# Mixture-of-experts tail on one core: one region of rows per expert, 39 tiles, and outputs added to memory by accumulating indirect DMAs

## The chip, the cores and the metric

One core of a Trainium2 (trn2) chip runs the whole program. The metric is the device time of one execution in microseconds (us), as the median of several runs. Engines are named as in the profile: PE (matmul), PEld (weight load), DVE, ACT, POOL and SP; a "q" behind a name is that engine's own instruction queue, which also issues DMAs.

## What is computed

Per batch of 512 rows (four batches, width 512), a linear attention over 1024 context rows, then a layer of eight experts, of which each row uses two:

```python
def _L0_ffn_ref(x, Wr, We, be):
    logits = jnp.einsum('bsd,de->bse', x, Wr)
    w, sel = jax.lax.top_k(logits, 2)
    w = jax.nn.softmax(w, axis=-1)
    gate = jnp.einsum('bsk,bske->bse', w, jax.nn.one_hot(sel, E, dtype=w.dtype))
    for e in range(E):
        out = out + gate[..., e:e + 1] * (jnp.einsum('bsd,df->bsf', x, We[e]) + be[e])

x = x + _L0_xattn_ref(_layernorm(x), ctx, Wq, Wg, bg, Wkv, Wo)
x = x + _L0_ffn_ref(_layernorm(x), Wr, We, be)
```

There are 2048 rows and so 4096 pairs of a row and an expert. Every matmul is in float32 precision, made of three passes over operands cut into a high and a low half (`three`: high by high, high by low, low by high).

## The kernel before, in words

**Attention.** Each engine has an instruction stream written by hand. The lists `KEYS` and `QUERIES` set the order of the steps of a batch. Batch by batch PE makes keys, values, queries, gate, attention and the output projection; DVE adds the residual into `x2`; POOL has the expert weights cut and stored in DRAM (`we_halves`) beside it. Two steps of batch b run within the keys of batch b+1: the logits with `pick_two` (the two experts of each row and their weights) and `rank_two` (the place of each pair among the pairs of its expert). POOL then scatters each normed row twice, by two indirect DMAs of 128 rows (`scatter`, L493), into `xs`: a region of rows per expert.

**Experts.** The pairs come in two groups, batches 0 to 2 and batch 3, with regions of their own. `plan` (DVE) works out on the device which expert and which rows each tile of 128 rows has: 31 tiles for group 0 and 15 for group 1, a fixed 46, enough for any routing. SP zeroes 128 rows behind each expert's last one (`pad`, eight stores per group). A tile goes through these steps:

- SP reads the tile's row from `tile_row`, waits for a free slot (two slots) and loads 128 rows (`load_tile`, L361).
- PE turns the tile (`turn_m`, L1165: four transposes); ACT copies out the high half (`high_m`, L716), DVE makes the low half (`low_m`, L810).
- PE does twelve matmuls of 512 columns (`expert`, L1098 to L1100).
- DVE adds the expert's bias into one of two slots of `y_sb` (`copy_y`, L1014), and ACT stores it to `y` in DRAM (`store_y`, L733).

The list `START` sets the order of the first 13 tiles, among which the normed rows of batch 3 are turned ("T", "z"), and their logits ("L") and places ("K") are made. After the last tile of group 0 is stored, POOL gathers the two expert rows of each token for 12 blocks of 128 tokens (`gather`, L598), DVE scales and adds both to the residual (`combine`, L1020 and L1024), ACT stores the block to the output (`store_out`, L737). These 12 blocks run beside the last 12 tiles. The four blocks of batch 3 come after the last tile.

**Loads before the experts.** In SP's queue stand, in this order: `load_halves(1)` to `(3)`, the eight pads, tiles 0 and 1, eight loads of the biases (L394), `load_halves(4)` and `(5)` (L374, 2 MB each, after the gate matmuls of the last batch), tile 2, tile 3, `load_halves(6)`, tile 4, `load_halves(7)`. POOL passes each arrival on (`halves_in`) to PE's `we_ready`.

## Time and profile before

| | |
|---|---|
| median of 3 runs | 607.82 us (605.88 to 607.92) |
| profiled execution: its own time | 602.09 us |
| its span on the core | 600.6 us |
| PE busy | 546.1 us (91%) |
| DVE, ACT, POOL busy | 320.0, 186.9, 166.9 us |
| DMA | 114.18 MB, mean 190 GB/s |
| mean granted TensorE clock | 0.968 |

The span runs from the first to the last instruction of the core; the profiled execution's own time is 1.49 us longer. PE's busy time is an overlap of pipelined matmuls, so the distance between starts says what one costs. All times within the trace are us from the span's start.

### The profile page before, as it was taken

To read this page: it belongs to the slowest core of one execution; us is meant where nothing else is said; L and a number is where in the kernel's file an instruction comes from. 1 tells how busy PE (TensorE), PEld (TensorE's weight loads), DVE (VectorE), ACT (ScalarE), POOL (GpSimd) and SP (SyncE) were. 2 spreads that over 40 slices of the span, in tenths; PEclk is the share of its full clock that TensorE was granted. 3 is DMA by queue.
4 is the path that set the end of the run, shared out by engine and by line. 5 is a ranking of instruction groups with operands and counts; after the bars stand their busy time and mean duration, and the time that the engine had idled before them with its cause. 6 is when DMAs were issued, how large, how long until landed. Compare 5 with 4: busy or idle time off the path is not lost.

```text
span 600.6 us, 12872 instructions
## 1 busy us (share of the span) xinstructions
PE 546.1 (91%) x4192; PEld 443.6 (74%) x4193; DVE 320.0 (53%) x857; ACT 186.9 (31%) x340; POOL 166.9 (28%) x194
## 2 busy tenths in 40 slices
PE   6999996999999999999999999994899999999850
PEld 4778785788878888877888887883678888877630
DVE  4463374356436727535746645770566544447744
ACT  5456321334532343443244343231111111111100
POOL 3014645403633131554040350010112000055413
PEclk9999999799999999999999999996899999999995
DMA  8813344632453062355052137789847568789946
GB/s 270 308 37 106 141 141 169 201 122 108 149 196 114 18 229 71 139 179 207 4 202 80 72 141 297 264 286 420 306 147 241 145 206 269 226 254 369 408 178 189
DMA packets 44446, 114.18 MB, mean 190 GB/s; under 512 B 4976, under 2 KB 4976, under 8 KB 43504
## 3 DMA queue, kind: packets, MB, share of 16 engines
q1 hardware_dynamic: 24240, 57.43, 28.6%
q0 software_dynamic: 11232, 39.85, 18.5%
q10 hardware_dynamic: 8928, 16.26, 7.1%
q8 instruction: 32, 0.52, 0.4%
q14 instruction: 14, 0.11, 0.1%
HBM read 66.86 MB, written 46.66 MB: 189 GB/s over the span
## 4 chain that ended last, share of the span: by engine, by line
PE 61%; DMA 12%; issue 5%; POOL 3%; SPq 3%; DVE 3%; ACT 1%; POOLq 0%; DVEq 0%; ACTq 0%
PE pj L1098 17%; PE pj L1100 17%; PE pj L1099 17%; DMA khat<-xs 5%; PE tp L1090 4%; PE tp L1165 3%; DMA out_dram<-wraw 1%; DMA wraw<-in_L_ffn_We_dram 1%; POOL aux L533 1%; PE pj L1185 1%; PE kvb L1157 1%; DMA we_halves<-aux 1%; PE pj L1107 1%; DMA qhat<-y,gidx 1%; SPq L365 1%
## 5 line engine op out<-in xcount | busy, mean ns | idle before, releaser
L1098 PE MATMUL pj<-R 128*128 128x512 f32 x448 | 185.6, 414 | 10.3 <-DVE R L806 9.3
L1100 PE MATMUL pj<-R 128*128 128x512 f32 x448 | 177.4, 396 | 0.0
L1099 PE MATMUL pj<-R 128*128 128x512 f32 x448 | 176.8, 395 | 0.0
L1098 PEld LDWEIGHTS pj<-R 128*128 128x128 f32 x448 | 85.4, 191 | 27.4 <-DVE R L806 10.3
L1100 PEld LDWEIGHTS pj<-R 128*128 128x128 f32 x448 | 85.2, 190 | 19.3
L1099 PEld LDWEIGHTS pj<-R 128*128 128x128 f32 x448 | 85.7, 191 | 15.4
L1098 PE MATMUL pj<-R,aux 128*128 x184 | 77.5, 421 | 5.5 <-issue 3.6
L1100 PE MATMUL pj<-R,aux 128*128 x184 | 73.2, 398 | 0.0
L1099 PE MATMUL pj<-R,aux 128*128 x184 | 73.0, 397 | 0.0
L716 ACT CAST aux<-tp 128x512 fp32r<-128x512 f32 x46 | 26.9, 585 | 121.6 <-PE tp L1165 114.5
L806 DVE TENSOR_TENSOR R<-tp,R 128x512 fp32r<-128x512 f32 x64 | 43.8, 684 | 24.9 <-ACT R L638 24.7
L871 DVE SCALAR_TENSOR_TENSOR khat<-buf,khat 128x512 f32<-128x512 f32 x32 | 25.1, 783 | 54.0 <-ACT buf L675 53.9
L500 POOL TENSOR_TENSOR rstd<-rstd,mhalf 128x1 f32<-128x1 f32 (+1 forms) x20 | 13.4, 669 | 126.7 <-DVE rstd L824 126.6
L1098 PEld LDWEIGHTS pj<-R,aux 128*128 128x128 f32 x184 | 35.4, 192 | 15.2 <-issue 9.0
L493 POOL DMA_INDIRECT xs<-normed,xidx x16 | 16.2, 1013 | 100.7 <-DVE xidx L859 98.3
L598 POOL DMA_INDIRECT qhat<-y,gidx x16 | 15.9, 995 | 95.2 <-issue 77.1
L810 DVE TENSOR_TENSOR aux<-tp,aux 128x512 fp32r<-128x512 f32 x46 | 31.7, 689 | 18.5 <-ACT aux L716 17.4
L1100 PEld LDWEIGHTS pj<-R,aux 128*128 128x128 f32 x184 | 35.3, 192 | 7.5
L1099 PEld LDWEIGHTS pj<-R,aux 128*128 128x128 f32 x184 | 35.4, 193 | 6.0
L638 ACT CAST R<-tp 128x512 fp32r<-128x512 f32 x64 | 37.7, 589 | 6.2 <-PE tp L1090 5.7
L1165 PE MATMUL tp<-ident,khat 128*128 128x128 f32 x184 | 28.6, 278 | 11.8 <-DMA khat<-xs 11.8
L533 POOL TENSOR_TENSOR aux<-wraw,aux 128x1024 fp32r<-128x1024 f32 x14 | 36.7, 2620 | 1.2
(158 smaller groups left out, 652.5 us busy)
## 6 DMA issues: line engine op xcount, KB each, us to landing
we_halves<-aux POOLq DMA_DIRECT2D x14, 1024.0 KB, 5.0
R<-we_halves SPq DMA_DIRECT2D x7, 2048.0 KB, 11.9
khat<-xs SPq DMA_DIRECT2D x46, 256.0 KB, 3.6
wraw<-in_L_ffn_We_dram POOLq DMA_DIRECT2D x16, 512.0 KB, 6.4
buf<-in_ctx_dram SPq DMA_DIRECT2D x15, 512.0 KB, 3.8
y<-kvbd ACTq DMA_DIRECT2D x23, 256.0 KB, 3.6
y<-zeros ACTq DMA_DIRECT2D x23, 256.0 KB
wraw<-in_x_dram SPq DMA_DIRECT2D x4, 1024.0 KB, 8.0
```

Source lines behind the costliest of these rows:

```text
L493: nc.gpsimd.indirect_dma_start(out=xs_dram[g][:, :], out_offset=bass.IndirectOffsetOnAxis(ap=xidx[:, t, j:j + 1], axis=0), in_=xn[t], in_o ...
L533: nc.gpsimd.tensor_tensor(aux[:, 2:4, :], e_raw[:, ks, :], aux[:, 0:2, :].bitcast(F32), ALU.subtract).then_inc(wx_low, 1)
L638: nc.scalar.copy(dst, src).then_inc(SEMS["h_" + kind], 1)
L716: nc.scalar.copy(xsT_hi[:, slot, :, :], tp[slot][:, :, :]).then_inc(MOE["h_m"], 1)
L806: nc.vector.tensor_tensor(lo, tp_bank("l_" + kind, i)[:, :, :], hi.bitcast(F32), ALU.subtract).then_inc(SEMS["l_" + kind], 1)
L810: nc.vector.tensor_tensor(xsT_lo[:, slot, :, :], tp[slot][:, :, :], xsT_hi[:, slot, :, :].bitcast(F32), ALU.subtract).then_inc(MOE["l_m"], 1)
L871: nc.vector.scalar_tensor_tensor(khat[:, i % 2, :], expk[:, i % 2, :], 1.0, khat[:, i % 2, :], ALU.min, ALU.add).then_inc(SEMS["khat"], 1)
L1090: last = nc.tensor.transpose(bank[:, k, :], src[:, k * P:(k + 1) * P], ident[:, :])
L1098: nc.tensor.matmul(bank[:, :], s_hi(k), m_hi(k), start=(k == 0), stop=False)
L1099: nc.tensor.matmul(bank[:, :], s_hi(k), m_lo(k), start=False, stop=False)
L1100: last = nc.tensor.matmul(bank[:, :], s_lo(k), m_hi(k), start=False, stop=(k == KT - 1))
L1165: last = nc.tensor.transpose(tp[slot][:, k, :], xs_raw[:, slot, k * P:(k + 1) * P], ident[:, :])
```

## The change

- `xs` is one region per expert for all four batches. A row is 528 floats wide: 512 values, the gates of the eight experts, the row's token number and a mark for padding. `x2_dram`, `y_dram`, the gathers, `combine` and `store_out` are gone. `store_x2` writes the residual straight into the output.
- There are 39 tiles. The first 17 (`M0`) are full ones from batches 0 to 2 (`plan_full`); `plan_rest` orders the other 22 when batch 3 is ranked. Pads are one block of 128 rows at the end of `xs` and one per expert.
- A tile's rows bring their gate and token: `pay` (DVE) takes the tile's expert from a table and copies the gate to `w_sel` and the token to `out_idx`. After `copy_y` ACT scales the result by the gate (`scale_y`), and POOL adds it to the output rows by one accumulating indirect DMA (`add_rows`).
- Tiles have four load slots (`XS`) and four result slots (`YS`). `copy_y(m)` waits until add m-4 has landed. Add m waits, with `tile_alone[m]` at 16, until the three before it have landed; with 0, only until those up to m-5 have. The first eight always wait. `tile_alone` is 16 for the first tile of an expert in either part (rows of two experts can have the same token), for the last one of an expert that has no tile in the first part, and for spare tiles.
- Rows that nothing uses in a tile point to tokens that the expert doesn't have (`mark_pads`, `find_pads`, step "C"), so that they add zeros harmlessly.
- The tile loops, the batch loop of DVE and the pad loop are written out. The biases come in two loads of 1 MB; the second is issued by ACT within `START` (its place is x's buffer). `load_halves(1)` and `(2)` are issued earlier, and four tiles are loaded ahead of `load_halves(4)`.

The diff, cut to its core:

```diff
-    GROUP_TILES = ((B - 1) * TT, TT)
-    ROWS = [n * P + P for n in GROUP_TILES]
-    TILES = [2 * n + E - 1 for n in GROUP_TILES]
...
+    W = D + 2 * E
+    GATES, TOKEN, PADDED = D, D + E, D + E + 1
+    ROWS = B * L + P
+    PAIRS = 2 * B * L
+    M0 = (2 * (B - 1) * L - E * (P - 1) + P - 1) // P
+    M_ALL = PAIRS // P + E - 1
...
+    XS, YS = 4, 4
...
+        for m in range(9, M_ALL):
+            START += tiles(m) + ([("C", "", 0)] if m == M0 - 2 else [])
...
+            def load_tile(m):
+
+                row = sp.value_load(tile_row[0:1, m:m + 1], min_val=0, max_val=E * ROWS)
+                if m >= XS:
+                    sp.wait_ge(MOE["t_m"], mth(m - XS))
+                    sp.wait_ge(paid, m - XS + 1)
+                sp.dma_start(xs_raw[:, m % XS, :], xs_dram[bass.ds(row, P), :]).then_inc(xs_loaded[m % XS], 16)
...
-            load_tile(0, 0, 0)
-            load_tile(0, 1, 1)
-            sp.wait_ge(SEMS["qhat"], nth("qhat", B - 1, G - 1))
-            for e in range(E):
-                sp.dma_start(be_all[:, e, :], be[e:e + 1, :].broadcast_to((P, D))).then_inc(be_loaded, 16)
+            for m in range(XS):
+                load_tile(m)
             sp.wait_ge(SEMS["g"], nth("g", B - 1, TT - 1))
             load_halves(4)
             load_halves(5)
-            load_tile(0, 2, 0)
+            load_tile(XS)
+            store_x2(B - 1)
             sp.wait_ge(SEMS["wo"], nth("wo", B - 1, TT - 1))
-            load_tile(0, 3, 1)
             load_halves(6)
-            load_tile(0, 4, 0)
+            load_tile(XS + 1)
             load_halves(7)
...
             halves_in(5)
             halves_in(6)
             halves_in(7)
...
+            def add_rows(m):
+
+                slot = m % YS
+                if m == 0:
+                    pool.wait_ge(x2_stored, 16 * B)
+                if m == M0:
+                    pool.wait_ge(x2_stored, 16 * B + 16)
+                pool.wait_ge(y_scaled, m + 1)
+                if m < 2 * YS:
+                    for d in range(1, min(m, YS - 1) + 1):
+                        pool.wait_ge(added[(m - d) % YS], 16 * ((m - d) // YS + 1))
+                else:
+                    alone = pool.value_load(tile_alone[0:1, m:m + 1], min_val=0, max_val=16)
+                    for d in range(1, YS):
+                        pool.wait_ge(added[(m - d) % YS], alone + 16 * ((m - d) // YS))
                 passed()
-                for j in range(2):
-                    nc.gpsimd.indirect_dma_start(out=yg[slot][j], out_offset=None, in_=y_dram[g][:, :],
-                                                 in_offset=bass.IndirectOffsetOnAxis(ap=gidx[:, slot, j:j + 1], axis=0)).then_inc(gathered[slot], 16)
+                nc.gpsimd.indirect_dma_start(out=out_rows[:, :], out_offset=bass.IndirectOffsetOnAxis(ap=out_idx[:, m % (2 * YS):m % (2 * YS) + 1], axis=0),
+                                             in_=y_sb[slot], in_offset=None, compute_op=ALU.add).then_inc(added[slot], 16)
...
+            for step, kind, i in START:
+                if step == "M":
+                    if i == M0 + 2:
+                        pool.wait_ge(planned, 2)
+                    if i >= 2:
+                        add_rows(i - 2)
+                elif step == "K":
+                    scatter(last, i)
...
+            def scale_y(m):
+
+                act.wait_ge(MOE["y_copied"], mth(m))
+                nc.scalar.activation(y_sb[m % YS], y_sb[m % YS], ACT.Identity, scale=w_sel[:, m % (2 * YS):m % (2 * YS) + 1]).then_inc(y_scaled, 1)
...
+                        act.dma_start(be_all[:, 4:8, :], be[4:8, :].rearrange("(a e) d -> a e d", a=1).broadcast_to((P, 4, D))).then_inc(be_loaded, 16)
...
+            def pay(m):
+
+                e = dve.value_load(tile_expert[0:1, m:m + 1], min_val=0, max_val=E - 1)
+                chosen[m] = e
+                n = m % (2 * YS)
+                row = xs_raw[:, m % XS, :]
+                nc.vector.tensor_scalar(w_sel[:, n:n + 1], row[:, bass.ds(e + GATES, 1)], 1.0, None, ALU.mult)
+                nc.vector.scalar_tensor_tensor(out_idx[:, n:n + 1], pad_token[:, bass.ds(e, 1)], row[:, PADDED:PADDED + 1], row[:, TOKEN:TOKEN + 1],
+                                               ALU.mult, ALU.add).then_inc(paid, 1)
...
+            def copy_y(m):
+
+                dve.wait_ge(MOE["m_done"], mth(m))
+                if m >= YS:
+                    dve.wait_ge(added[m % YS], 16 * (m // YS))
+                nc.vector.tensor_tensor(y_sb[m % YS], pj[m % 2][:, :], be_all[:, bass.ds(chosen[m], 1), :].rearrange("p a d -> p (a d)"), ALU.add).then_inc(MOE["y_copied"], 1)
 
-            dve.wait_ge(be_loaded, 16 * E)
+            dve.wait_ge(be_loaded, 32)
```

**POOL's queue at the start of the experts.** Before, behind the last batch's norms (L500, L501), POOL waits for the weights and scatters batch 3's rows:

```order
L585 MEMSET bias 128x512 [waits wx_loaded2,wx_loaded3,wx_loaded4,wo]
L493 DMA xs<-normed,xidx 5120x512 [waits wx_loaded5,wx_loaded6,wx_loaded7,slot]
L493 DMA xs<-normed,xidx 5120x512
L493 DMA xs<-normed,xidx 5120x512 [waits slot]
L493 DMA xs<-normed,xidx 5120x512
L493 DMA xs<-num,xidx 5120x512 [waits slot]
```

Now the adds (L590) stand there, and the scatters (L479) between them:

```order
L590 DMA out_dram<-khat,out_idx 2048x512 [waits wx_loaded2,wx_loaded3,wx_loaded4,wx_loaded5,wx_loaded6,wx_loaded7,x2_stored,y_scaled]
L590 DMA out_dram<-khat,out_idx 2048x512 [waits y_scaled,added0]
L479 DMA xs<-normed,xidx 17536x528 [waits slot]
L479 DMA xs<-normed,xidx 17536x528
L590 DMA out_dram<-buf,out_idx 2048x512 [waits added0,y_scaled,added1]
L590 DMA out_dram<-buf,out_idx 2048x512 [waits added0,added1,y_scaled,added2]
L479 DMA xs<-normed,xidx 17536x528 [waits slot]
```

The wait for all the weights' halves stood ahead of the first scatter; it now stands ahead of the first add. Later adds read `tile_alone` first, on the same engine:

```order
L586 TENSOR_LOAD tile_alone [waits y_scaled]
L586 ISA x2
L588 REGISTER_ALU
L588 REGISTER_ALU [waits added0]
L590 DMA out_dram<-khat,out_idx 2048x512 [waits added3,added2]
L586 TENSOR_LOAD tile_alone [waits y_scaled]
```

**SP's queue where the last weights are loaded.** Before (L361 tile, L374 halves):

```order
L374 DMA R<-we_halves 128x4096 [waits g]
L374 DMA R<-we_halves 128x4096
L359 TENSOR_LOAD tile_row
L359 ISA x2
L361 ISA [waits t_m]
L361 DMA khat<-xs 128x512
```

Now (L366 tile, L371 halves, L332 residual):

```order
L332 DMA out_dram<-gate 128x4x512 [waits x2]
L371 DMA R<-we_halves 128x4096 [waits wx_stored,wo]
L362 TENSOR_LOAD tile_row
L362 ISA x2
L366 ISA [waits paid,t_m]
L366 DMA buf<-xs 128x528
L371 DMA R<-we_halves 128x4096 [waits wx_stored]
```

The last load of halves stands behind the load of tile 5, which now waits for `paid` too.

## Rows read from the trace of the kernel before

**Rows 1.** The page: busy times, and the chain that ended last by engine.
```profile
PE 546.1 (91%) x4192; PEld 443.6 (74%) x4193; DVE 320.0 (53%) x857; ACT 186.9 (31%) x340; POOL 166.9 (28%) x194
...
PE 61%; DMA 12%; issue 5%; POOL 3%; SPq 3%; DVE 3%; ACT 1%; POOLq 0%; DVEq 0%; ACTq 0%
```

**Rows 2.** Busy time by stretch: length, each engine's busy us (count), PE clock, DMA share, GB/s.
```profile
400.00:420.00 20.00, 10.99 (x75) 8.51 (x76) 4.77 (x14) 3.65 (x6) 1.98 (x5) 0.74 1.03 417
...
460.00:480.00 20.00, 19.64 (x98) 16.13 (x97) 11.87 (x30) 3.52 (x6) 0.00 (x0) 1.00 0.56 160
...
540.00:560.00 20.00, 17.57 (x81) 13.29 (x80) 15.29 (x29) 2.94 (x5) 11.59 (x13) 1.00 1.02 379
...
580.00:600.60 20.60, 0.00 (x0) 0.00 (x0) 6.39 (x9) 0.00 (x0) 8.12 (x8) 0.56 0.56 175
```

**Rows 3.** PE in order of time, two tiles' transposes: start, length, instruction [idle before].
```profile
484.61 0.60 PE L1165 MATMUL tp<-ident,khat 128*128 128x128 f32 x4
487.79 0.60 PE L1165 MATMUL tp<-ident,khat 128*128 128x128 f32 x4
```

**Rows 4.** The same view: the two waits of PE for a tile, and matmuls behind them.
```profile
414.20 1.12 PE L1165 MATMUL tp<-ident,khat 128*128 128x128 f32 x4 [9.01 <-DMA khat<-xs]
...
430.93 0.65 PE L1165 MATMUL tp<-ident,khat 128*128 128x128 f32 x4 [2.41 <-DMA khat<-xs]
...
433.12 0.63 PE L1098 MATMUL pj<-R,aux 128*128 x1
433.55 0.63 PE L1099 MATMUL pj<-R,aux 128*128 x1
```

**Rows 5.** The same view: the transposes of two tiles beside the combining, the last one's included.
```profile
539.45 0.60 PE L1165 MATMUL tp<-ident,khat 128*128 128x128 f32 x4
...
572.04 0.60 PE L1165 MATMUL tp<-ident,khat 128*128 128x128 f32 x4
```

**Rows 6.** All engines in order of time, the end of the program.
```profile
577.71 0.39 PE L1100 MATMUL pj<-R,aux 128*128 x1
578.24 0.69 DVE L1014 TENSOR_TENSOR zeros<-pj,buf 128x512 f32<-128x512 f32 x1 [1.77 <-PE pj L1100]
...
582.02 0.94 POOL L598 DMA_INDIRECT qhat<-y,gidx  x1 [14.24 <-DMA y<-zeros]
```

**Rows 7.** The line of the scatters (L493), then that of the gathers (L598): issue to landing.
```profile
L493 POOL DMA_INDIRECT xs<-normed,xidx x16: 954/982/1112, 137.0 to 444.7; - x16
DMA to landing us min/median/max: 2.7/3.3/5.7
...
DMA to landing us min/median/max: 3.3/5.7/7.3
```

**Rows 8.** POOL in order of time: an indirect DMA behind another, and one that DVE released.
```profile
331.73 0.98 POOL L493 DMA_INDIRECT xs<-normed,xidx  x1 [0.30 <-issue]
...
541.59 1.20 POOL L598 DMA_INDIRECT qhat<-y,gidx  x1 [0.30 <-DVE gidx L943]
```

**Rows 9.** The chain that ended last, in order of time: DVE's index, and its table load.
```profile
541.06 0.10 DVE gidx L943
...
541.34 0.82 DVEq L1011
```

**Rows 10.** DVE in order of time, one steady tile; and ACT's scaling of 128 rows.
```profile
475.48 0.69 DVE L1014 TENSOR_TENSOR zeros<-pj,buf 128x512 f32<-128x512 f32 x1 [1.57 <-PE pj L1100]
...
405.27 0.82 ACT L648 ACTIVATE num<-gate,shift,rstd 128x512 f32<-128x512 f32 x1
```

**Rows 11.** DMA issues: tensor, queue, count, KB each, median us to landing.
```profile
wraw<-in_x_dram SPq DMA_DIRECT2D x4, 1024.0 KB, 8.0
```

**Rows 12.** The line of the halves' loads (L374): issue to landing.
```profile
DMA to landing us min/median/max: 8.6/11.9/17.5
```

More of the change, by code:

```diff
@@ L583, in _ @@
             halves_in(4)
-            pool.wait_ge(SEMS["wo"], nth("wo", last, TT - 1))
-            nc.gpsimd.memset(bias[:, :], 0.0).then_inc(zeroed, 1)
             halves_in(5)
@@ L588, in _ @@
             halves_in(7)
-            for t in range(TT):
-                scatter(1, last, t)
-            def gather(g, c, slot):
-                pool.wait_ge(gidx_done, c + 1)
-                pool.wait_ge(combined, c + 1)
-                passed()
-                for j in range(2):
-                    nc.gpsimd.indirect_dma_start(out=yg[slot][j], out_offset=None, in_=y_dram[g][:, :],
-                                                 in_offset=bass.IndirectOffsetOnAxis(ap=gidx[:, slot, j:j + 1], axis=0)).then_inc(gathered[slot], 16)
@@ L618, in _ @@
+            for step, kind, i in START:
[6 more added lines that the diff above has]
+                    scatter(last, i)
+            add_rows(M_ALL - 2)
+            add_rows(M_ALL - 1)
+            for s in range(YS):
+                pool.wait_ge(added[s], 16 * ((M_ALL - 1 - s) // YS + 1))
         @block.scalar
@@ L859, in rank_two @@
-                nc.vector.scalar_tensor_tensor(xidx[:, t, :], idf[:, t, 0:2], float(ROWS[g]), rank_t[:, :], ALU.mult, ALU.add).then_inc(SEMS["slot"], 1)
+                nc.vector.scalar_tensor_tensor(xidx[:, t, :], idf[:, t, 0:2], float(ROWS), rank_t[:, :], ALU.mult, ALU.add).then_inc(SEMS["slot"], 1)
                 dve.wait_ge(SEMS["slot"], nth("slot", b, t))
+                if b == 0 and t < 2:
+                    nc.vector.tensor_copy(early[:, t, :], pos[:, :])
+                    nc.vector.tensor_copy(early_members[:, t, :], members[:, t, :])
+                    nc.vector.tensor_copy(early_run[:, :], run[:, :]).then_inc(kept, 1)
+                    dve.wait_ge(kept, t + 1)
@@ new lines, in mark_pads @@
+            def mark_pads():
+                tokens = token[:, :].rearrange("p (t e) -> p t e", e=1).broadcast_to((P, 2, E))
+                link(nc.vector.tensor_scalar(early_run[:, :], early_run[:, :], -1.0, float(2 * P), ALU.mult, ALU.add))
+                link(nc.vector.tensor_tensor(member_place[:, :, :], early[:, :, :], over(early_run[:, :], 2), ALU.add))
+                link(nc.vector.tensor_tensor(early[:, :, :], tokens, early[:, :, :], ALU.subtract))
+                link(nc.vector.tensor_tensor(early[:, :, :], early[:, :, :], member_place[:, :, :], ALU.subtract))
+                link(nc.vector.scalar_tensor_tensor(list_place[:, :, :], early_members[:, :, :], 0.0, early[:, :, :], ALU.is_equal, ALU.mult))
+                link(nc.vector.tensor_tensor(list_place[:, :, :], list_place[:, :, :], member_place[:, :, :], ALU.add))
+                dve.wait_ge(x2_stored, 16 * B + 16)
+                yield
+                for t in range(2):
+                    for e in range(E):
+                        last = nc.vector.tensor_scalar(marks[:, t, e, :], place_p[:, :], list_place[:, t, e:e + 1], None, ALU.is_equal)
+                    last.then_inc(pads_marked, 1)
+                    yield
```

460 lines of the change are left out of this document (197 added, 263 removed).

## The prediction

> **What bounds the kernel now.** I read the page first: PE is busy for 91% of the span, and 61% of the chain that ended last is PE [rows 1]. DVE, ACT and POOL are far from full. So PE's tiles count, and then every stretch in which PE doesn't run. The table by stretch shows three of them [rows 2]: at 400 to 420 (11 of 20 us busy, DMA engines full), at 540 to 560 (17.6 of 20) and from 580 on (nothing).
>
> PE in order of time gives the price of a tile: the transposes of two neighbours start 3.18 us apart, with no idle time noted [rows 3]. The busy time would say more, since pipelined matmuls overlap in it. Beside the combining, the eight tiles from 539.45 to 572.04 take 32.59 us [rows 5] where 8 x 3.18 = 25.4 would do: 7.2 lost. PE waits for tiles twice early on, 9.01 and 2.41 us, and behind each wait matmuls start 0.43 us apart [rows 4], against about 0.23 (3.18 less the transposes, by twelve). The last matmul ends at 577.71 + 0.39 = 578.1 [rows 6], and the remaining 22.5 us are the gathers, additions and stores of batch 3.
>
> **The change on PE.** 46 tiles become 39: 7 x 3.18 = 22.3 us less. The combining is gone, so its 7.2 go too. The wait of 2.41 and the seven slow matmuls behind it (7 x 0.2 = 1.4) go: tiles are loaded up to three ahead of their use. The wait of 9.01 does not go, though tile 2 is now loaded ahead of the weights. DVE waits for both bias loads before it makes tile 1's low half, and the second load is issued by ACT behind its last normalizing activation, which ends at 405.27 + 0.82 = 406.1 [rows 10]. A load of 1 MB lands after 8.0 us [rows 11]: 414.1, about when tile 2 came before. I count no gain and no loss there.
>
> Costs: two tiny DVE operations per tile in `pay`, 0.25 us. In a steady tile DVE idles 1.57 us before the bias addition [rows 10], and the table load of 0.82 [rows 9] stood in there already, so they are hidden; in the eight tiles with logits or places that gap is mostly used, and I count 0.3 each. With the new plan's steps and the 16 small matmuls of step C I take 3.5 us in all (nothing at least, 8 at most). Attention is left alone: wider rows, a few more constants on POOL, earlier weight loads, all beside a busy PE. PE then ends at 578.1 - 22.3 - 7.2 - 3.8 + 3.5 = 548.3.
>
> **The adds.** Behind a product stand: start and length of the bias addition (0.14 + 0.69), the scaling (0.1 + 0.82 [rows 10]), POOL's table load, taken as DVE's 0.82 [rows 9], and the start of a released indirect DMA, 541.59 - 541.16 = 0.43 [rows 8, 9]. That is 3.0 us, then L, the time from an add's start to its landing. No row shows an accumulating DMA. From below L is the fastest scatter, 2.7; from above a loaded gather and a scatter one after the other, 5.7 + 3.3 = 9.0 [rows 7]. It is the same instruction to the same kind of memory as the scatter (3.3), so I start there and add a second read. Two transfers of 256 KB per tile keep the DMA engines busy for a share of 0.56 [rows 2], so one is 0.56 x 3.18 / 2 = 0.9 us; a read from DRAM costs the gather 0.6 more at its fastest than the scatter [rows 7]. 3.3 + 0.9 = 4.2 without that, 4.8 with it: I take **L = 4.5**.
>
> An add that waits can start L + 0.45 after the one before; at 4.5 that is 4.95, against 3.18 for a tile. **So adds, not PE, set the end if enough of them wait.** I counted the reference's choices for these inputs. Over all batches the experts have 493, 494, 567, 549, 499, 537, 580 and 377 pairs: 4, 4, 5, 5, 4, 5, 5, 3 tiles, 35 in all, and 4 of the 39 are spare. Of batches 0 to 2 the first part takes 3, 2, 3, 2, 2, 2, 3 and 0. Waiting are adds 1 to 7, then 8, 10, 12, 14, then 17, 18, 20, 22, 25, 27, 30, 32, 34, and the spare 35 to 38: 24. The other 14 cost POOL its own time: 0.96 + 0.30 [rows 8] + 0.82 = 2.08 each.
>
> The first add has a wait of its own. In POOL's queue it stands behind the arrival of all weights. The last load of halves stands behind tile 5's load, which needs `paid` of tile 1, and that needs the biases: 414.1 + 0.69 + 0.82 + 0.25 = 415.9, issue at 416.5, and the fastest such load took 8.6 [rows 12]: 425.1. Waiting adds follow at once, since products 0 to 3 are there by then. End = 425 + 24 x 0.45 + 14 x 2.08 + 25 L = 464.9 + 25 L, which at 4.5 is **577.4**. DVE's wait for a free result slot then holds PE back by some us, which changes nothing more, as the adds are the later ones. The batch 3 scatters between them run while an add is on its way.
>
> Against the profiled execution's span of 600.6 that is -23.2. Of the expected gain on PE (29.8) and in the tail, the adds take back about 23. With 1.49 around the span its own time would be 578.9 where before has 602.09. The median of the runs lies 5.73 above that, and I keep this difference: **584.6 us**.
>
> One rule of the Trainium skill would give less. "DMA: Bandwidth & Descriptors" (Anatomy of one DMA) fits a POOL-issued DMA as about 2.0 us fixed plus bytes / 436e3; with 256 KB read twice that is 3.2 us, and by it the sum would be the first rival's. The scatter's row is above its 2.6 for one read. The same page (Rules for kernel authors) says that an accumulate must wait for any earlier access of the same bytes. That speaks against the change's gain, for it is the wait that is priced here, and no run here shows the loss that it warns of.
>
> **Rivals.**
>
> - *The adds keep up.* With L at 3.3, as a lightly loaded scatter, a waiting add costs 3.75, and pairs of waiting and free ones average under 3.18. Then PE sets the end: 548.3 + 3.0 + 3.3, and the five last adds in a row lose 5 x 0.57 = 2.9: span 557.5, time 564.7. It decides below L = 3.7, where 464.9 + 25 L meets 557.5. For it: the scatters' median is 3.3. Against: a second read must be made somewhere.
> - *Dear adds, still a gain.* L of 5.0 to 5.4: 597 to 607.
> - *Slower: adds longer than two tiles' work hides.* One mechanism: each waiting add is a round trip to DRAM and back within one DMA, and 25 of them stand in a row. From L = (600.6 - 464.9) / 25 = 5.43 on the kernel is slower. At 6.0 it is 614.9 + 7.2 = 622. For it: gathers landed after 5.7 at the median, 7.3 at most, under load [rows 7]; against: that was in the stretch with a DMA share of 1.02 and two gathers per block [rows 2], and here a tile has one load and one add.
> - *The relaxed waits don't relax.* If all adds waited, 425 + 38 x 4.95 + 4.5 = 617.6, so 624.8. The table's rule frees 14 of them, so this needs the plan to fail.
>
> **Chances.** Forecast (L of 3.7 to 5.0): 0.45. Adds keep up: 0.21. Dear but faster: 0.07. Within 0.5% of before (L of 5.3 to 5.55; about what a measurement of this kernel can tell from no change): 0.04. Slower by dear adds: 0.20. All wait: 0.03. Faster by over 0.5%: 0.45 + 0.21 + 0.07 = 0.73; slower 0.23. The range goes from 561 (L at its lower bound of 2.7: 548.3 + 3.0 + 2.7 = 554, plus 7.2) to 622 (L = 6.0). Above it lie the upper end of L, 9.0, and the last rival.
>
> **What would show it.** Right: adds whose issue to landing is near 4.5 us at the median; POOL waiting for `added` before most of them; DVE's bias addition released by a DMA; PE's tiles at 3.18 only in places, and PE's last matmul near 555; the first add near 425; 16 or more us between the last matmul and the end, all adds. PE's first long wait stays, released through DVE by the bias load. Wrong: a landing below 3.7 with the end about 9 us behind PE's last matmul (first rival), or above 5.4. Also wrong would be a first add near 410, which takes up to 15 us off the chain, or a PE that waits for weights or tiles and not for result slots.

## The result and the profile after

The changed kernel took **621.38 us** (median of 4 runs, 618.41 to 622.99), and the kernel before 607.87 beside it (605.88 to 609.63): ratio **1.0212, 95% interval 1.0183 to 1.024**. It is slower, where 584.6 and faster was forecast. The range reached to 622.0 and so just held the time; the sign was wrong. The profiled execution took 621.42 us with a span of 619.9. A few executions of before were disturbed and longer; the ratios and the times of before given here leave them out.

The page of the changed kernel, the rows that answer to [rows 1]:

```profile
PE 528.5 (85%) x4096; PEld 428.4 (69%) x4096; DVE 304.1 (49%) x912; ACT 208.8 (34%) x372; POOL 197.7 (32%) x215
...
DMA 12%; PE 5%; issue 4%; SPq 2%; POOLq 1%; POOL 1%; DVE 1%; ACT 0%; DVEq 0%
DMA out_dram<-khat,out_idx 6%; DMA out_dram<-buf,out_idx 6%; PE pj L1099 2%; PE pj L1101 1%; PE pj L1100 1%; POOLq L586 1%; POOL out_dram L590 1%; PE tp L1166 1%; SPq L401 1%; SPq L402 1%; DMA buf<-xs 0%; POOL xs L479 0%; SPq L362 0%; POOLq L588 0%; POOLq L427 0%
```

PE's busy time fell by 17.6 us, but the span grew by 19.3. The chain could be followed back only over the last quarter of the span, and there it is mostly adds: their two result tensors stand first with 12% of the span together, PE has 5%. Before, 61% of it was PE.

The table by stretch, with the columns of [rows 2]:

```profile
400.00:420.00 20.00, 9.54 (x40) 7.41 (x37) 4.16 (x12) 4.00 (x7) 0.73 (x2) 0.67 0.82 308
460.00:480.00 20.00, 10.13 (x36) 7.41 (x35) 14.30 (x53) 3.34 (x5) 8.27 (x6) 0.84 0.59 116
480.00:500.00 20.00, 9.32 (x37) 7.54 (x38) 3.99 (x16) 2.41 (x4) 4.65 (x3) 0.61 0.76 194
...
580.00:600.00 20.00, 6.24 (x29) 4.56 (x26) 2.77 (x6) 2.75 (x4) 6.20 (x4) 0.78 0.42 53
600.00:619.90 19.90, 0.00 (x0) 0.00 (x0) 0.00 (x0) 0.00 (x0) 3.10 (x2) 0.50 0.32 40
```

From 460 to 500 PE is busy for half the time (before, 19.64 of 20 at 460 to 480), and the last 20 us hold two adds and nothing else.

The line of the adds (L590): durations on POOL, what POOL waited for ahead of them, who waited for them, and issue to landing:

```profile
L590 POOL DMA_INDIRECT out_dram<-khat,out_idx x20: 1549/1551/1679, 424.8 to 603.7; - x20
L590 POOL DMA_INDIRECT out_dram<-buf,out_idx x19: 1549/1551/1608, 438.0 to 609.2; - x19
its engine sat idle before it (us, times) until:
  DMA out_dram<-khat,out_idx: 38.2, 9
  DMA out_dram<-buf,out_idx: 30.2, 8
...
  DVE buf L1046: 31.9, 12
  DVE khat L1046: 17.3, 6
DMA to landing us min/median/max: 4.7/5.3/6.3
```

An add lands 5.3 us after its start at the median, where the scatter of the same size took 3.3 [rows 7], and 4.7 to 4.9 where it is alone, as at the end of the program. DVE's bias addition stood 18 times, 49 us in all, behind the landing of an add, waiting for its result slot.

The chain in order of time, two steps between waiting adds near the end: start, length, what.

```profile
592.29 4.85 DMA out_dram<-buf,out_idx
597.14 0.02 issue
597.17 0.04 POOLq L427
597.21 0.54 issue
597.75 0.21 POOLq L586
597.96 4.84 DMA out_dram<-khat,out_idx
```

From the landing to the next start are 597.96 - 597.14 = 0.82 us (0.81 to 0.89 in the four such steps at the end). Most of it, 0.54 + 0.21, comes behind the last of the waits and the semaphore increment (L427).

POOL in order of time, adds 10 to 13 and then 35 to 38:

```profile
480.88 1.55 POOL L590 DMA_INDIRECT out_dram<-buf,out_idx  x1 [4.98 <-DMA out_dram<-khat,out_idx]
482.74 1.55 POOL L590 DMA_INDIRECT out_dram<-buf,out_idx  x1 [0.30 <-issue]
494.55 1.55 POOL L590 DMA_INDIRECT out_dram<-khat,out_idx  x1 [10.26 <-issue]
500.23 1.57 POOL L590 DMA_INDIRECT out_dram<-khat,out_idx  x1 [4.13 <-DMA out_dram<-khat,out_idx]
...
592.29 1.55 POOL L590 DMA_INDIRECT out_dram<-buf,out_idx  x1 [4.16 <-DMA out_dram<-buf,out_idx]
597.96 1.55 POOL L590 DMA_INDIRECT out_dram<-khat,out_idx  x1 [4.12 <-DMA out_dram<-buf,out_idx]
603.69 1.55 POOL L590 DMA_INDIRECT out_dram<-khat,out_idx  x1 [4.18 <-DMA out_dram<-khat,out_idx]
609.23 1.55 POOL L590 DMA_INDIRECT out_dram<-buf,out_idx  x1 [3.99 <-DMA out_dram<-khat,out_idx]
```

The spare adds at the end stand 5.5 to 5.7 us apart, and a free add follows its predecessor by 1.86. That isn't all gain: the waiting add behind a free one takes 5.8 to 7.7 us (add 12 aside). It waits for adds that are under way together, and such adds land after up to 6.3 us. Add 12 comes 11.81 us behind add 11. Its reason is in three other views: PE's waits, SP's queue, and DVE and ACT in order of time.

```profile
414.85 0.79 PE L1099 MATMUL pj<-R,aux 128*128 x1 [10.46 <-issue]
...
490.68 1.12 PE L1166 MATMUL tp<-ident,buf 128*128 128x128 f32 x4 [16.73 <-DMA buf<-xs]
```

```profile
476.44 9.60 SPq L402 DMA_DIRECT2D xs<-zeros  x8
487.93 12.01 SPq L366 DMA_DIRECT2D buf<-xs  x6
```

```profile
477.69 0.69 DVE L1046 TENSOR_TENSOR khat<-pj,wraw 128x512 f32<-128x512 f32 x1 [0.85 <-DMA out_dram<-khat,out_idx]
...
491.83 0.58 ACT L705 CAST aux<-tp 128x512 fp32r<-128x512 f32 x1 [18.53 <-PE tp L1166]
492.31 0.72 ACT L723 ACTIVATE khat<-khat,w_sel 128x512 f32<-128x512 f32 x1
```

PE waits 16.73 us for tile 14. Its load stands in SP's queue behind the wait for the second plan and behind eight pads of 1.2 us each. The plan itself was late by an add: its last steps stand on DVE behind tile 11's bias addition, which waited for add 7 to land. The forecast had no such wait. Add 12 meets it through ACT. Its product had its bias at 478.4, but ACT's scaling of it stands behind the high half of tile 14, and so came at 492.3. Whether the scaling ahead of the high half would have freed add 12, no run tried.

### The profile page after: what moved, and what is told of

It is laid out like the page before. It is cut to its first block and busy times, and to the rows that moved or that the text cites. A ratio compares the mean times of both kernels' runs of the same rounds, so it can differ in the third digit from the quotient of the medians.

```text
span 619.9 us, 11964 instructions
## 1 busy us (share of the span) xinstructions
PE 528.5 (85%) x4096; PEld 428.4 (69%) x4096; DVE 304.1 (49%) x912; ACT 208.8 (34%) x372; POOL 197.7 (32%) x215
## 5 line engine op out<-in xcount | busy, mean ns | idle before, releaser
L1099 PE MATMUL pj<-R,aux 128*128 x156 | 68.6, 440 | 29.2 <-issue 17.3
L1101 PE MATMUL pj<-R,aux 128*128 x156 | 65.0, 417 | 0.0
L1100 PE MATMUL pj<-R,aux 128*128 x156 | 64.3, 412 | 0.0
L590 POOL DMA_INDIRECT out_dram<-khat,out_idx x20 | 31.3, 1564 | 83.8 <-DMA R<-we_halves 21.8
L1099 PEld LDWEIGHTS pj<-R,aux 128*128 128x128 f32 x156 | 31.5, 202 | 38.3 <-issue 32.6
L590 POOL DMA_INDIRECT out_dram<-buf,out_idx x19 | 29.6, 1560 | 52.8 <-DMA out_dram<-khat,out_idx 24.7
L705 ACT CAST aux<-tp 128x512 fp32r<-128x512 f32 x39 | 22.7, 583 | 63.8 <-PE tp L1166 57.7
L776 DVE TENSOR_TENSOR aux<-tp,aux 128x512 fp32r<-128x512 f32 x39 | 26.7, 685 | 27.9 <-ACT aux L705 15.3
L1166 PE MATMUL tp<-ident,buf 128*128 128x128 f32 x156 | 24.3, 279 | 16.7 <-DMA buf<-xs 16.7
L479 POOL DMA_INDIRECT xs<-normed,xidx x16 | 17.0, 1062 | 67.1 <-DVE xidx L823 64.1
L661 ACT ACTIVATE khat<-pj 128x512 f32<-128x512 f32 x32 | 19.1, 597 | 53.8 <-PE pj L1101 53.8
L668 ACT COPY buf<-pj 128x512 f32<-128x512 f32 x32 | 18.8, 587 | 52.0 <-PE pj L1101 50.3
```

The lines of the kernel that those rows point to most:

```text
L590: nc.gpsimd.indirect_dma_start(out=out_rows[:, :], out_offset=bass.IndirectOffsetOnAxis(ap=out_idx[:, m % (2 * YS):m % (2 * YS) + 1], axis=0),
L661: nc.scalar.activation(khat[:, i % 2, :], pj_bank("expk", i)[:, :], ACT.Relu)
L668: nc.scalar.copy(vones[:, i % 2, :, 0:HD], pj_bank("v_copied", i)[:, :].rearrange("p (g c) -> p g c", g=HEADS)).then_inc(SEMS["v_copied"], 1)
L705: nc.scalar.copy(xsT_hi[:, slot, :, :], tp[slot][:, :, :]).then_inc(MOE["h_m"], 1)
L776: nc.vector.tensor_tensor(xsT_lo[:, slot, :, :], tp[slot][:, :, :], xsT_hi[:, slot, :, :].bitcast(F32), ALU.subtract).then_inc(MOE["l_m"], 1)
L1099: nc.tensor.matmul(bank[:, :], s_hi(k), m_hi(k), start=(k == 0), stop=False)
```

## Where the 42.5 us lie

The forecast span was 577.4, as 425.0 (first add) + 24 waiting steps + 14 free steps + L. By the starts of the 39 adds in the trace:

| part | forecast | measured | difference |
|---|---|---|---|
| first add | 425.0 | 424.76 | -0.2 |
| 24 waiting steps | 24 x 4.95 = 118.8 | 153.99 | +35.2 |
| 14 free steps | 14 x 2.08 = 29.1 | 30.48 | +1.4 |
| last add's start to the end | 4.5 | 10.67 | +6.2 |
| span | 577.4 | 619.9 | +42.5 |

Of the 35.2, 24 x 0.42 = 10 are the start behind a landing (0.87 where 0.45 was forecast). Add 12's step has another 11.81 - 4.5 - 0.87 = 6.4. The remaining 18.7 are close to 24 x 0.8 = 19, L at its median of 5.3 and not 4.5. The free steps only look right: twelve took 1.86 and not 2.08, 2.7 us less, but add 13, late behind add 12, came after 5.68, and add 16 after 2.52.

## The experiments

The runs were made in several sets, each with its own runs of before. Before took between 599.8 and 610.7 us at the median from one set to the next, once 599.8 and once 609.6 on the same chip, while a kernel with adds repeated there gave 614.4 and 613.8. So I compare kernels with adds by their own times, and take ratios only where before itself is the question. Between two sets even these own times can differ by some 3 us: three sets gave 620.5 to 622.6 for the changed kernel, and 610.6 and 607.3 stand below for two kernels whose adds wait alike.

| kernel | own time, us | last add starts | ratio to before (95%) |
|---|---|---|---|
| the changed kernel, second and third time | 620.5, 622.6 | 606.4, 609.9 | 1.0185 (1.0142 to 1.0228), 1.0224 (1.0151 to 1.0297) |
| plain scatter in place of the add | 578.5 | 569.0 | 0.9617 (0.9554 to 0.968) |
| every add waits | 666.5 | 655.4 | 1.109 (1.1017 to 1.1163) |
| adds apart, none waits | 576.8 | 565.3 | 0.9602 (0.9539 to 0.9664) |
| tiles 14 to 16 ahead of the pads | 614.4, 613.8 | 604.1, 600.1 | 1.0218, 1.0077 |
| table from add 1 | 616.3 | 605.1 | 1.0109 (1.0074 to 1.0144) |
| three edits | 610.6 | 598.7 | 1.0019 (0.9996 to 1.0041) |
| and spare blocks (edit had no effect) | 607.3 | 594.7 | 1.0125 (1.008 to 1.0171) |
| bias wait moved | 617.0 | 604.8 | 1.0289 (1.0249 to 1.0329) |
| last waits on ACT | 617.0 | 608.2 | 1.0278 (1.0243 to 1.0313) |
| all edits, spare adds still waiting | 601.4 | 591.7 | 1.0026 (0.9997 to 1.0055) |
| **all edits, spare adds free** | **593.4** | 580.6 | **0.976 (0.9704 to 0.9816)** |
| and pads between the loads | 594.0 | 579.2 | 0.9738 (0.9709 to 0.9767) |
| product side, two versions (2 runs each) | 576.5, 573.2 | 567.6, 564.4 | 0.9467, 0.9389 |

**What of L is the accumulation.**

```diff
-  in_=y_sb[slot], in_offset=None, compute_op=ALU.add).then_inc(added[slot], 16)
+  in_=y_sb[slot], in_offset=None).then_inc(added[slot], 16)
```

> The changed kernel with one word less: the indirect DMA of add_rows writes its rows in place of adding them (the additions to what is there are left out, and the output with them); waits, table and everything else stay. In the changed kernel an add lands 4.84 to 4.93 us after its start when alone (median 5.3 over all) and occupies POOL for 1.55 us; steps that wait are 5.7 us. Theory A (the second read inside the DMA and the longer issue make L what it is): L falls to the unloaded scatter's 3.3, POOL's time per instruction to 0.96, a waiting step to about 3.3 + 0.87 = 4.2; 24 x 1.5 = 36 us less on the chain, less what the stretch of PE's 16.7 us wait keeps: 585 to 595 us. Theory B (traffic beside it and the way of the semaphore set L): L stays at 4.5 to 5.3 and the time at 612 to 621.

Its line of adds, and the chain between two waiting ones:

```profile
L590 POOL DMA_INDIRECT out_dram<-buf,out_idx x19: 954/958/962, 434.4 to 569.0; - x19
...
DMA to landing us min/median/max: 2.7/2.7/5.1
```

```profile
558.40 2.67 DMA out_dram<-buf,out_idx
561.07 0.02 issue
561.10 0.04 POOLq L427
561.14 0.76 issue
561.90 2.66 DMA out_dram<-khat,out_idx
```

Theory A holds, and more strongly than stated, as 578.5 us lie below its 585 to 595: the accumulation costs 4.7 - 2.7 = 2.0 us from issue to landing (alone) and 1.55 - 0.96 = 0.59 us of POOL. The 0.83 us from landing to the next start is there with a plain scatter too, so it belongs to the released issue and not to the add. A waiting step is 3.5 us here, near the tile's 3.2, and PE is busy for 20.00 of 20 us in each stretch from 480 to 560: below L = 3.7 PE sets the end, as the first rival had it. Its last matmul starts at 563.0. The waiting adds at the very end still trail by some 3 us, which is also what that rival had. 578.5 is what is left if adds cost no more than scatters.

**All adds waiting.**

```diff
-  if m < 2 * YS:
+  if True:
       for d in range(1, min(m, YS - 1) + 1):
           pool.wait_ge(added[(m - d) % YS], 16 * ((m - d) // YS + 1))
```

> The changed kernel with every add waiting for the three before it, on constants; the table isn't read. If the adds' chain sets the time and the table frees 14 of them in truth: 38 steps of 5.73 us are 217.7 us against the 153.99 + 30.48 = 184.5 measured, so +33 us: about 650 to 657 us. If PE, the tiles' loads or DVE set the pace and the adds only follow: 621 to 627 us. If a wait on a register or the table load costs by itself: less than 650, since both are gone here.

45 us more than the changed kernel: the adds' chain sets the time, and the table does free its 14. The forecast of 33 was low, since a step here is (655.37 - 425.15) / 38 = 6.06 us on average and not 5.73:

```profile
534.39 1.55 POOL L590 DMA_INDIRECT out_dram<-buf,out_idx  x1 [4.64 <-DMA out_dram<-khat,out_idx]
540.72 1.55 POOL L590 DMA_INDIRECT out_dram<-buf,out_idx  x1 [4.78 <-DMA out_dram<-buf,out_idx]
```

Here 6.33 us apart. From 606.1 on, when the last tile load had been issued, they were 5.5 to 5.7: from 500 to 605 the landings took 5.5 to 5.7 at the median, behind that 4.7. The prediction's 624.8 for this case, by its L of 4.5, was 42 us too low for the same reasons as the forecast.

**Adds apart: the product side by itself.**

```diff
-  nc.gpsimd.indirect_dma_start(out=out_rows[:, :], ...
+  nc.gpsimd.indirect_dma_start(out=y_dram[slot][:, :], ...
```

(with four blocks `y_dram`, and without the waits for other slots' adds)

> The changed kernel with each of the four result slots adding into a block of memory of its own, and no wait of one add for another (the sum of x2 and the experts' rows is left out of the output). DVE still waits for a slot's add before it fills the slot again. What is left is the product side: PE, the bias loads, the plan, the pads, one DMA per tile. Theory A (only the waits between adds hold the time): PE ends near 555, the last add lands 8 us later, 5.6 us of empty end: 565 to 575 us. Theory B (the product side is itself late, by the two long waits of PE, 10.5 and 16.7 us, and the adds share DMA engines): 585 to 600 us. Theory C (adds are slow in any order, POOL's 1.55 us and landing above 6 us): 600 or more.

576.8 us, just above A's 565 to 575, and PE's last matmuls start at 562.6, not 555. So 45 of the changed kernel's 621 us are the waits between adds and what they delay. But the product side is 14.7 us later than the forecast's 548.3 for PE's end. PE's longer waits in this kernel:

```profile
414.19 0.79 PE L1093 MATMUL pj<-R,aux 128*128 x1 [10.15 <-issue]
...
477.05 1.12 PE L1160 MATMUL tp<-ident,buf 128*128 128x128 f32 x4 [12.45 <-DMA buf<-xs]
```

The bias wait was in the sum, the 12.45 for tile 14 wasn't. Behind it matmuls start 0.43 us apart again, and tile 14's transposes are followed by the next after 5.29 us and not 3.20. By this the wait for tile 14 would be 12.45 + 2.1 = 14.6 of the 14.7, an estimate from these rows. From 480 on PE is busy without a gap, at 3.2 us for a tile, as forecast.

**Tiles ahead of the pads.**

```diff
-  for m in range(XS + 2, 14):
+  for m in range(XS + 2, M0):
       load_tile(m)
   sp.wait_ge(planned, 2)
   (eight pads)
-  for m in range(14, M0):
-      load_tile(m)
```

> The changed kernel with the loads of tiles 14 to 16 issued before SP's wait for the second plan and before the eight pads. In the changed kernel PE waits 16.73 us for tile 14 and add 12 starts 11.81 us behind add 11, 6 more than a usual step, add 13 3.8 late. Theory A (this wait is on the adds' chain): 8 to 11 us less, 610 to 613. Theory B (tile 17 is then late by the same amount, since it still stands behind the pads): 618 to 622. Theory C (the adds behind it would have caught up): 619 to 622, with the long wait gone.

614.4 us lie between the theories' ranges, the ratio to before was the same 1.02, and the unedited kernel wasn't in this set. So here it is again, beside one:

> Tiles 14 to 16 loaded before the second plan and the pads, once more beside the unchanged kernel. Its span was 614.6 us on the other chip, against 619.9 for the changed kernel on the first, and add 13 came 8 us earlier, add 38 5 us. Theory A (the pads' wait is on the adds' chain, and half of it is lost again by later products): 4 to 7 us less than the changed kernel on this chip. Theory B (difference of chips only): within 1.5 us of it.

> The changed kernel unchanged, on the same chip as the runs beside it, since the kernel before took 599.8 us on the chip of the last four runs against 607.9 on the first. Expected: a ratio to before of 1.018 to 1.024 as at first. If the chain of adds, which holds no clock of TensorE and little traffic, is what sets the time, its own time should differ less between the chips than that of before: then a ratio above 1.024 where before is fast.

Of the unedited kernel 620.5, with the edit 613.8: 6.8 us less, theory A. The last add comes at 600.1 and not 606.4. Add 12 came at 490.0 where it was at 494.5, add 13 at 491.8 where it was at 499.9.

**The table from add 1 on.** Each slot's semaphore is first raised once by a tiny DMA of 64 bytes.

```diff
-  if m < 2 * YS:
-      (waits for the three before, on constants)
-  else:
-      alone = pool.value_load(tile_alone[0:1, m:m + 1], ...)
-      for d in range(1, YS):
-          pool.wait_ge(added[(m - d) % YS], alone + 16 * ((m - d) // YS))
+  if m >= 1:
+      alone = pool.value_load(tile_alone[0:1, m:m + 1], ...)
+      for d in range(1, min(m, YS - 1) + 1):
+          pool.wait_ge(added[(m - d) % YS], alone + 16 * ((m - d) // YS) + 16)
```

> The changed kernel, but the plan's table decides from add 1 on, not from add 8: adds 1, 2, 4, 6 and 7 no longer wait (to keep each wait's value positive every slot's semaphore is raised once by a tiny DMA before). Each of these five steps is 5.7 us now and 1.86 if free. Theory A (adds set the pace from the first on): add 11 comes 12 to 19 us earlier, DVE's second plan ends earlier too since result slots are free, and the end comes 10 to 15 us earlier. Theory B (tile 14's load behind the pads sets add 12 whatever stands before): add 12 comes at most 4 us earlier and the end 0 to 4.

POOL's rows of adds 10 to 13:

```profile
474.45 1.55 POOL L593 DMA_INDIRECT out_dram<-buf,out_idx  x1 [4.49 <-DMA out_dram<-khat,out_idx]
476.30 1.55 POOL L593 DMA_INDIRECT out_dram<-buf,out_idx  x1 [0.30 <-issue]
491.37 1.57 POOL L593 DMA_INDIRECT out_dram<-khat,out_idx  x1 [13.51 <-issue]
495.95 1.56 POOL L593 DMA_INDIRECT out_dram<-khat,out_idx  x1 [3.02 <-DMA out_dram<-khat,out_idx]
```

Add 11 comes 6.0 us earlier, half of A's least. But in this execution everything was late already before the experts (SP's first load of halves is issued at 358.6, and at 355.6 in the unedited kernel's trace). Counted from the first add, add 11 comes 9.7 us earlier. Adds 2, 4, 6 and 7, now free, don't follow after 1.86 us: each stands in POOL's queue behind two scatters of batch 3, and 4.5 us behind what went before (451.84, two scatters, 456.31, two scatters, 460.77). While an add was waited for, these scatters were hidden, as the prediction had it. Of a freed step they are what is left. Add 12 is 3.1 earlier and the whole 4.2: that is theory B (just over its 4), the pads' wait swallows the rest. An expected gain went into a wait that stood behind it.

**Three edits**: both of these, and the wait for the weights of experts 5 to 7 moved behind add 3.

> Three edits at once: the table from add 1 on, tiles 14 to 16 loaded before the second plan and the pads, and the wait for the last three experts' weights (halves 5 to 7) moved behind add 3 in POOL's queue, so that the first add can start when its product is there, about 4 us earlier. Theory A (the chain of adds is all that holds the time, 18 of 38 adds still waiting): the end 20 to 28 us earlier than the changed kernel, near or below the kernel before. Theory B (PE's side, whose end was 563 of 575.6 with adds apart, becomes the bound in the middle): 12 to 20 us earlier.

9.9 us less, less than either theory gave. The first add started at 418.7 and not 424.3, but the second at 426.6: ACT scaled its product only at 424.13 to 424.86, since PE's matmuls for it stand behind the bias wait and the scaling behind the next tile's high half.

**The bias wait.** One line of DVE's queue, moved:

```diff
-  dve.wait_ge(be_loaded, 32)
   planning, marking = plan_rest(bias), mark_pads()
...
       elif step == "M":
+          if i == 0:
+              dve.wait_ge(be_loaded, 32)
           copy_y(i)
```

> The changed kernel with one line moved: DVE waits for the biases in front of the first bias addition and no longer in front of tile 1's low half and of its weights and row numbers. In the changed kernel this wait holds PE for 10.5 us (tile 1's products), and the last load of weights with it, since tile 5's load stands ahead of it and waits for tile 1's numbers; the first add was at 424.3. Theory A (my account of the first add): the last weights are issued about 10 us earlier, the first add comes at 414 to 419, adds 1 to 11 by 4 to 9 us earlier; by the pads' wait at add 12 some of it is lost: 2 to 7 us less in the end. Theory B (the weights' load was late for its own reasons, DMA engines at 0.8 busy): the first add within 2 us of 424, the end within 2.

SP issued the last halves at 402.99 and not at 415.67, 12.7 us earlier, so the account of the first add was right as to the order. It had missed what else moves: issued so early, the load runs beside the second bias load (issued at 402.5) and the previous load of halves (issued at 400.0), with a DMA share of 0.99 from 405 to 415, and from its issue to the first add are 17.1 us instead of 9.1. DVE still waited 11.6 us for the biases, now in front of tile 0's addition, and PE 8.0 us behind it. The first add came at 420.1, just outside A's window, and the last at 604.8: against 608.2 with the next kernel in the same set 3.5 us less, but the own times are equal (617.0), as that kernel saves 2.5 us at its end. So A: some 3.5 to 4.5 us, inside its 2 to 7.

**The empty end.**

```diff
-  for s in range(YS):
-      pool.wait_ge(added[s], 16 * ((M_ALL - 1 - s) // YS + 1))
+  (the same four waits, on ACT, behind scale_y(M_ALL - 1))
```

> The changed kernel, but the last waits, for the landing of the last four adds, are ACT's and not POOL's. In the changed kernel and in every run of mine there are 5.6 to 5.8 us without any work between the last landing and the end of the span, with the kernel before about 2. Theory A (something that POOL does at its end, behind its last wait, takes them): 3 to 5 us less. Theory B (whoever waits, what lies between a landing of POOL's queue and the end is the same): within 1 us.

From the last add's start to the end of the span: 616.3 - 608.24 = 8.1 us, against 10.4 to 10.7 in three runs of the changed kernel (10.67, 10.64, 10.4). About 2.5 us go, less than A's 3 to 5, and the rest stays. The own time of 617.0 is 3.5 to 5.6 less than the changed kernel's in three other sets, which by itself would be A; the traces show only 2.5 of it at the end.

**Spare adds apart, then all edits.** First the three edits, with spare adds meant to go to disjoint blocks of rows (a marker column in the pad rows adds 256 k to the token of spare tile k). Then the same with the bias wait moved and the last waits on ACT:

> The kernel of the three edits, and besides the spare tiles' adds (35 to 38, which add a weight of zero times something to rows of batch 0) go to disjoint blocks of 256 rows, so that of the four only the first waits. Add 34 was issued 22 us before add 38 in the kernel of the three edits: four steps of 5.5. Theory A (these steps are the end): three of them fall from 5.5 to about 1.9, less what the last, now in traffic of three, lands later (about 1): 9 to 11 us less than with the three edits, about 600 where before takes 610 (ratio 0.98 to 0.99). Theory B (products of the spare tiles come late, PE's side holds the end): 0 to 5 us less.

> All edits together: table from add 1 on, tiles 14 to 16 ahead of the pads, last weights behind add 3, spare adds disjoint, the wait for the biases in front of the first bias addition, the last waits on ACT. If each gives what its theory A says, about 7 to 10 us beyond the kernel with disjoint spare adds: 590 to 595 where before takes 610, ratio 0.967 to 0.975. If the chain of adds and PE's side now bound each other by turns: 596 to 602, ratio 0.975 to 0.985.

In both, adds 35 to 38 still stood 5.4 to 5.7 us apart: the edit hadn't freed them. A second rule of the plan, that the last tile of an expert without tiles in the first part waits, is written with "at least", and marks every tile behind it too. What the first shows against the three edits (607.3 and 610.6) is thus no gain by freed adds; the two stood in different sets. The second is 601.4, within its theory B. The repair is one comparison:

```diff
-  tile_u, tile_u, -1.0, tile_b, ALU.is_ge, ALU.mult
+  tile_u, tile_u, -1.0, tile_b, ALU.is_equal, ALU.mult
```

> All edits together once more, with the second rule of the plan made exact, so that of the spare adds 35 to 38 only 35 waits; in the last run with all edits all four still did, at 5.5 to 5.7 us each, and the last add was issued at 591.7 of a span of 599.4. Theory A (these steps are the end): adds 36 to 38 follow at 1.9 us or as their products come, the last add is issued at 580 to 582, lands later by about 1 us, and the span is 588 to 591: own time 589 to 593, 1 to 3% below before, which took 600 to 610. Theory B (their products or the slots hold them): last add at 586 or later, 596 or more.

> The changed kernel once more, beside these two. Its own time was 621.4 and 620.5 us so far, before 607.9, 599.8, 609.6 and 600.0 in four calls. Theory A (before varies, the chain of adds doesn't): own time 618 to 622 whatever before takes. Theory B (all kernels vary together): own time moves by the same per cent as before.

```profile
569.58 1.55 POOL L592 DMA_INDIRECT out_dram<-buf,out_idx  x1 [4.77 <-DMA out_dram<-khat,out_idx]
575.04 1.55 POOL L592 DMA_INDIRECT out_dram<-buf,out_idx  x1 [3.91 <-DMA out_dram<-buf,out_idx]
576.89 1.55 POOL L592 DMA_INDIRECT out_dram<-khat,out_idx  x1 [0.30 <-issue]
578.75 1.55 POOL L592 DMA_INDIRECT out_dram<-khat,out_idx  x1 [0.30 <-issue]
580.60 1.55 POOL L592 DMA_INDIRECT out_dram<-buf,out_idx  x1 [0.30 <-issue]
```

593.4 us, 8.0 less than with the four waiting (in another set; in the traces the last add starts 11.1 us earlier), and 29.2 less than the changed kernel beside it (622.6). **It beats before: 0.976 (0.9704 to 0.9816).** The last spare adds now follow at 1.85 us as A had it, and the time is just above A's 589 to 593. The changed kernel's third time fits theory A of its text within 0.6 us: its three own times lie within 0.3% of each other, and before's went from 599.8 to 610.7.

**The product side once more.** Adds apart with all the other edits:

> Adds apart in four blocks of memory and none waiting for another (the sum of x2 and the experts' rows is left out), and besides tiles 14 to 16 ahead of the pads, the last weights behind add 3, DVE's wait for the biases in front of the first bias addition, the last waits on ACT. With adds apart alone PE ended at 563 and the span was 575.6. Theory A (pads 10 us, bias wait 5, end 3): PE ends at 548 to 553, as the forecast's 548.3 had it, span 557 to 563. Theory B (the eleven tiles with logits, places and scatters are slow by themselves): PE ends at 556 or later, span 566 or more.

PE ends even later (565.2), so A falls: its transposes for tile 17 wait instead, whose load SP issues at 486.0. Between 438 and 467 PE also stood still four times for about 2 us, 8.5 in all, where with adds apart alone it did once, for 2.0.

```profile
488.74 1.11 PE L1160 MATMUL tp<-ident,buf 128*128 128x128 f32 x4 [7.38 <-DMA buf<-xs]
```

Then with the pads' rows announced by themselves, and two pads behind each of the loads of tiles 11 to 14:

```diff
+  if m == 11:
+      sp.wait_ge(pads_at, 1)
+  if 11 <= m < 15:
+      pad(2 * m - 22)
+      pad(2 * m - 21)
```

> The last kernel with adds apart (sum of x2 and experts' rows left out of the output), but the eight pads no longer wait for the second plan: DVE announces their rows by themselves, at the plan's first instruction, and SP issues them two by two behind the loads of tiles 11 to 14. Theory A (the tile behind the pads is late by them, about 7.4 us of waiting plus some 3 of slow clock): PE ends at 553 to 557, span 563 to 567. Theory B (the second plan itself or the last scatters hold tile 17): PE ends at 562 to 565, span 572 to 575.

> The kernel of the last all-edits run, 593.4 us, with the pads moved in the same way. There PE waited 6.7 us for tile 17, adds 15 to 17 stood 4.8 and 5.6 us apart where add 16 needn't wait for another. Theory A (that wait is on the chain of adds): 2 to 4 us less, 589 to 591.5, ratio to before 0.96 to 0.975. Theory B (the chain catches up, add 17 waits for a landing anyway): within 1.5 us of 593.4.

```profile
467.99 1.11 PE L1166 MATMUL tp<-ident,buf 128*128 128x128 f32 x4 [8.80 <-DMA buf<-xs]
```

Now tile 12 waits, for 8.8 us, behind the pads' announcement, and the short waits come to 6.4 us. PE ends at 562.0: B. In the complete kernel it makes no difference either (594.0 and 593.4), B again. So the wait moved from tile 14 to 17 to 12, and PE's end from 563.0 to 565.2 to 562.0. What the long wait lost, short ones took; for most of them the profile shows nothing that ended them, and no run tried them. A place for the pads that costs nothing wasn't found; what PE's end would be without them stays open.

## Why the prediction was wrong, point by point

- **What sets the end** was right: the chain of adds, not PE. All waiting is +45 us; none waiting is -45.
- **Number of waiting adds, 24 of 38, and the first add at 425** were right (424.76, with DVE waiting 12.0 us for the bias load as described, and POOL for the last weights). There is luck in the 425: ACT issued the bias load at 403.6 and not at 406.1, and it landed after 10.3 us and not 8.0.
- **L = 4.5** is the term that failed first. It measured 4.7 to 4.9 alone, 5.3 at the median and up to 6.3 with other adds under way, so one number for all waiting steps was wrong too. The forecast added 1.2 us to the scatter for a second read. The accumulation cost 2.0 over the same scatter, and 0.6 more of POOL, of which the forecast had nothing. The base of 3.3 was itself a loaded value; alone the scatter takes 2.7. Two errors that partly cancelled.
- **L + 0.45** failed with it: from a landing to the next start are 0.8 to 0.9 us. I had taken 0.43 from an indirect DMA released by DVE's semaphore [rows 8, 9]. Over 24 steps this is 10 us, beside the 20 of L: by the sum's own form, 464.9 + 24 x 0.42 + 25 x 5.3 = 607.5.
- **"PE end 548.3"** failed too: 562.6 + 0.4 with adds apart. The pads between tile loads were put at nothing. They were in the diff, in a queue that I had read; the text itself named "a PE that waits for tiles" as a sign against it, and PE did, for 16.73 us. In the changed kernel this cost 6.8 us in the end, by the run with tiles 14 to 16 ahead of the pads.
- **The end of the program** was taken as the last landing. 5 to 6 us follow it. That PE's last matmul starts near 555 was wrong by more than the pads: 588.8, since PE waited for result slots.
- **The 5.73 us** added for the medians had no ground: it is how before's profiled run lay below its median, and before's time wanders by more from one set of runs to the next. The changed kernel's median is its profiled time. This error hid 5.7 of the 42.5, and the forecast was 36.8 low.
- **The rivals.** "Slower: adds longer than two tiles' work hides" happened, at 622, by its mechanism: each waiting add a round trip. It was to need L above 5.43; the gap of 0.87 and the pads made 5.3 enough. The range held because of it. "Adds keep up below L = 3.7" held when L was made 2.7. "All wait" was right as a mechanism and 42 us low in price.
- **The two rules of the Trainium skill.** In the Trainium skill, the fit of "DMA: Bandwidth & Descriptors" (Anatomy of one DMA), 2.0 us plus bytes / 436e3, gives an estimate of 2.6 for the plain scatter of 256 KB, and 2.7 was measured; for the add, read twice, it gives an estimate of 3.2, and 4.7 was measured. The trace agrees for the write and not for the accumulation. The rule of the same page to wait before an accumulate (Rules for kernel authors) is what makes the chain; no run here left out such a wait on shared rows.

The likely gain on PE was real in part: with adds apart the kernel is 4% faster than before. The chain of adds took all of it and 2% more.

## What to carry to other kernels

Before a wait between DMAs is put into a loop, price the whole round trip by itself: issue, landing with the operation it will have, and the released issue. Multiply by the number of waits that the data make, and count spare and constant cases first, since they can be freed without touching the data. A tile that is loaded ahead of its use is only as early as what stands in the queue ahead of it: read each queue in order around every new small transfer, and each engine's own list of steps too, since a finished product can stand behind a step for a later tile. And when an edit takes a cost out, look in the trace whether it did: here one edit freed nothing, the last four adds still waited, and its 8 us appeared when a single comparison was changed.

## What I hadn't expected of the hardware

- An indirect DMA that adds occupies POOL for 1.55 us, the plain one for 0.96 (same 128 rows of 2 KB), and lands after 4.7 us against 2.7 at the fastest.
- The last load of weights, issued at 415.7, let the first add start 9.1 us later; issued at 403.0, beside the second bias load and the halves before it, 17.1 us later. Issuing it 12.7 us earlier gained 4 to 6.
- Between the last add's start and the end of the span lie 10.7 us, of which about 4.7 are its landing; moving the last waits from POOL to ACT took about 2.5 off. What the rest is, no run shows.
- The kernel before varied by 1.8% at the median between sets of runs, the changed kernel by 0.3%. Why before wanders, no run shows.
